# Two setup stages merged into the stages before them, and a layer norm whose variance and root stay in PSUM

## What is computed

```python
x = x + _L0_conv_ref(_gn(x), ...)      # layer 0
x = x + _L1_conv_ref(_gn(x), ...)      # layer 1

def _gn(v, G=32, eps=1e-5):            # per image, groups of 3 channels
    g = v.reshape(B_, G, C_ // G, H_, W_)
    m, s = mean(g, (2, 3, 4)), var(g, (2, 3, 4))
    return ((g - m) / sqrt(s + eps)).reshape(v.shape)

def _layernorm(x, w, b):               # over the 96 channels of a pixel
    return (x - m) / sqrt(v + EPS) * w + b

# L0: tok = windows of _gn(x); y = _layernorm(tok, norm1_w, norm1_b); q, k, v = y @ wq, y @ wk, y @ wv; ...
# L1: value, feat = 1x1 convolutions of _gn(x); centers = mean of feat over quarters of eight regions;
#     every pixel goes to the most similar centre of its region and head; aggregate, distribute, project
```

## Time and profile before

| | us |
|---|---|
| runs, median (lowest to highest) | 6937.62 (6933.67 to 6956.9) |
| profiled execution | 6937.03 |
| its span, first to last instruction | 6935.3 |
| group norm statistics (0 to the last aggregation) | 138.2 |
| attention setup and spreading of scale and shift, until the first load of the layer norm | 31.5 |
| first load of the layer norm to its first instruction on ACT | 15.3 |
| layer norm, first instruction on ACT to the first load of the attention | 448.5 |
| cluster setup, its first DMA to the cluster stage's first | 46.4 |

### The profile page before, as it was taken

How to read it: one execution, slowest core, us unless ns; L and a number is a source line. 1 busy time by engine, 2 the same in 40 slices (tenths; PEclk the granted TensorE clock), 3 DMA queues, 4 the chain that set the end, 5 groups by cost and what they waited for, 6 DMA issues and landing times. The chain is left out here.

```text
span 6935.3 us, 135783 instructions
## 1 busy us (share of the span) xinstructions
PE 6015.5 (87%) x51768; PEld 3118.6 (45%) x51768; DVE 5209.9 (75%) x7712; ACT 3497.3 (50%) x5182; POOL 2286.0 (33%) x4080
## 2 busy tenths in 40 slices
PE   0885999999999999999999689989998666578887
PEld 0332555555555555555555233335555111066663
DVE  7686888888888888888888455558887445456666
ACT  0553666666666666666666356644443111144431
POOL 0343455555554555555554656610000000000000
PEclk9997999999999999999999799999999788789987
DMA  7786344444444444444443598888987999835667
GB/s 306 192 240 179 72 106 101 101 104 106 103 108 100 103 109 102 105 101 101 107 96 71 146 269 235 237 288 345 345 341 266 283 314 316 249 90 167 189 183 248
DMA packets 761666, 1252.65 MB, mean 181 GB/s; under 512 B 159364, under 2 KB 477828, under 8 KB 730948
## 3 DMA queue, kind: packets, MB, share of 16 engines
q1 hardware_dynamic: 700532, 1090.77, 55.8%
q10 hardware_dynamic: 54560, 111.50, 5.3%
q0 software_dynamic: 5936, 41.68, 1.7%
HBM read 680.81 MB, written 508.40 MB: 171 GB/s over the span
## 5 line engine op out<-in xcount | busy, mean ns | idle before, releaser
L801 DVE TENSOR_REDUCE at_mz<-at_ps 128x4 bf16<-128x1024 f32 x1444 | 1772.3, 1227 | 105.3 <-PE at_ps L720 80.3
L668 ACT ACTIVATE at_E<-at_ps 128x1024 f32<-128x1024 f32 x1444 | 1399.4, 1021 | 382.6 <-PE at_ps L732 368.0
L732 PE MATMUL at_ps<-at_qaug,at_k 32*128 32x256 f32 x11552 | 830.0, 401 | 23.7 <-DVE at_qaug L842 23.7
L743 PE MATMUL at_ps<-at_E,at_vaug 128*32 128x256 f32 x11552 | 774.3, 385 | 5.5
L1282 PE MATMUL cv_ps<-cv_yin,cv_band 128*128 128x384 f32 x2304 | 745.4, 486 | 26.2 <-DMA cv_yin<-y_mlp 26.2
L1302 DVE TENSOR_TENSOR cv_yin<-cv_gl,cv_yin 64x384 f32<-64x384 f32 x1152 | 637.6, 553 | 150.3 <-ACT cv_gl L1293 142.4
L732 PEld LDWEIGHTS at_ps<-at_qaug,at_k 32*128 32x128 f32 x11552 | 523.0, 184 | 494.1 <-issue 384.5
L590 POOL TENSOR_TENSOR at_share<-at_rden,t_share 128x8 f32<-128x8 f32 x722 | 148.5, 206 | 1445.5 <-DVE at_rden L812 1445.5
L1282 PEld LDWEIGHTS cv_ps<-cv_yin,cv_band 128*128 128x128 f32 x2304 | 436.1, 189 | 335.7 <-DMA cv_yin<-y_mlp 27.1
L720 PE MATMUL at_ps<-at_k,at_q 32*128 32x256 bf16 x5776 | 574.2, 275 | 8.9 <-DMA at_k<-at_packed 7.4
L1293 ACT ACTIVATE cv_gl<-cv_ps,cv_bias 128x384 f32<-128x384 f32 x576 | 335.1, 582 | 435.8 <-PE cv_ps L1282 435.8
(11 more groups left out here) (217 smaller groups left out, 9596.0 us busy)
## 6 DMA issues: line engine op xcount, KB each, us to landing
cv_yin<-y_mlp SPq DMA_DIRECT2D x48, 2340.0 KB, 14.8
s_mlp<-cv_yin SPq DMA_DIRECT2D x48, 2340.0 KB, 8.4
at_rows_in<-y_attention SPq DMA_DIRECT2D x76, 768.0 KB, 6.1
gn_xin<-in_x SPq DMA_DIRECT2D x16, 3072.0 KB, 23.2
ln_xin<-in_x SPq DMA_DIRECT2D x192, 256.0 KB, 7.4
y_attention<-ln_xin SPq DMA_DIRECT2D x192, 256.0 KB, 3.8
cl_xu<-x SPq DMA_DIRECT2D x128, 384.0 KB, 3.6
at_xr<-in_x SPq DMA_DIRECT2D x68, 672.0 KB, 5.7
```

What stands on the lines that cost most here:

```text
L668: act.activation(E[:, m % 2, 2 * p:2 * p + 2, :], psum[:, 2 + 2 * p:4 + 2 * p, :], ACT.Exp).then_inc(exp_done, 1)
L732: i = pe.matmul(psum[:, 2 + h, TOK * j:TOK * j + TOK], k[rows, n % 2, tokens(w, 128 * j, 128)], qaug[rows, m % 2, :], start=True, stop=True)
L743: i = pe.matmul(pv_ps[32 * h:32 * h + VC, 0:TOK], vaug[:, m % 2, z, h, :], E[:, m % 2, h, z * TOK:(z + 1) * TOK], start=(z == 0), stop=(z ...
L801: dve.tensor_reduce(mz[:, m % 2].rearrange("p j (h c) -> p h j c", c=32)[:, 2 * p:2 * p + 2, :, DQ], psum[:, 0:2, :].rearrange("p h (j n) ...
```

## The change

1. Buffers, weights and the early loads of the layer norm are shared (norm_tables). The group norm's statistics are taken in the layer norm's own six tiles; the 16 loads of attention_setup go on ACT's queue inside group_norm_statistics, and SP issues the first two tiles of the layer norm there (LN_EARLY). The first image is aggregated in the middle.
2. gn_scale and gn_shift are spread over the partitions by three matmuls and two DVE copies in attention_setup, instead of 24 DMAs.
3. In the layer norm the variance stays in its PSUM bank. ACT takes Ln of a pair of chunks (two banks, 1024 columns) into SBUF and writes Exp back into the same banks, and DVE scales a chunk with the bank as operand, six chunks behind the centring. DVE's copy of the variance is gone. PE sums the squares two chunks behind instead of one; POOL has three buffers.
4. fc2 no longer waits for its stores; cluster_setup's SP does. The 18 loads and the memsets of cluster_setup are issued by POOL at fc2's start.
5. In cluster_setup 64 small DVE instructions become 8, the copies of means and weights go to POOL, two of the four copies of c_value_centres to ACT.

```diff
 def group_norm_statistics(nc, x, p, vdr, t, s):
+            for k in range(LN_EARLY):
+                sp.wait_ge(taken, STEPS + k - XB + 1)
+                norm_load(sp, x, s, k)
...
+            act.wait_ge(cleared, 4)
+            for to, of in setup_weights(p, t, s):
+                act.dma_start(to, of).then_inc(s["weights_loaded"], 16)
...
+                if m % PART == PART - 1:
+                    b, n = m // PART, PART * PER
+                    dve.wait_ge(taken, m + 1)
+                    dve.bn_aggr(t["mean_var"][:, b, :], stats[:, b * n:(b + 1) * n, :]).then_inc(aggregated, 1)
 def attention_setup(nc, p, t, s):
+            pool.wait_ge(s["weights_loaded"], LOADED)
+            for grp in range(CGRP):
+                pool.tensor_copy(s["spread"][:, grp, :].rearrange("p (g c) -> p g c", g=4),
+                                 t["eye"][0:C, 32 * grp:32 * grp + 32].unsqueeze(1).to_broadcast([C, 4, 32])).then_inc(spread_done, 1)
...
-            pe.matmul(ps[0:C, 3, 0:B], t["centre"][:], t["gn_shift"][:], start=True, stop=True).then_inc(pch, 1)
+            for grp in range(CGRP):
+                m = pe.matmul(ps[:, 3, 4 * grp:4 * grp + 2 * B], s["spread"][:, grp, :], t["gn"][:].rearrange("p a b -> p (a b)"), start=True, stop=True)
...
+            for b in range(B):
+                half = slice(64 * b, 64 * b + 64)
+                link(dve.tensor_copy(s["affine"][half], ps[half, 3, 0:4 * CGRP].rearrange("p (s a b) -> p a s b", a=2, b=B)[:, :, :, b]))
 def layer_norm(nc, x, y, p, t, s):
+    PAIR, PAIRS = 2, 3
+    LAG = PAIR * PAIRS
...
-                for g in range(4):
-                    for to, of in ((scale, t["gn_scale"]), (shift, t["gn_shift"])):
-                        sp.dma_start(to[32 * g:32 * g + 32, grp:grp + 1], of[32 * grp:32 * grp + 32, g // 2:g // 2 + 1]).then_inc(w_loaded, 16)
...
             def variance(n):
                 pe.wait_ge(sq_done, n + 1)
-                if n >= 2:
-                    pe.wait_ge(var_out, n - 1)
+                if n >= LAG:
+                    pe.wait_ge(z_done, n - LAG + 1)
...
+            for n in range(N + 2):
                 if n < N:
                     mean(n)
-                if n:
-                    variance(n - 1)
+                if n >= 2:
+                    variance(n - 2)
...
+            def roots(j):
+                banks = slice(root(PAIR * j), root(PAIR * j) + PAIR)
+                act.wait_ge(var_done, PAIR * (j + 1))
+                act.activation(logs[:, j % 2], psum[:, banks, :], ACT.Ln, bias=t["eps5"][:]).then_inc(log_done, 1)
+                act.wait_ge(log_done, j + 1)
+                act.activation(psum[:, banks, :], logs[:, j % 2], ACT.Exp, scale=-0.5).then_inc(rs_done, 1)
+            for n in range(XH_AHEAD):
+                affine(n)
+            for n in range(N + LAG):
+                if n + XH_AHEAD < N:
+                    affine(n + XH_AHEAD)
+                j = (n - LAG + PAIR) // PAIR
+                if n % PAIR == 0 and 0 <= j < N // PAIR:
+                    roots(j)
...
-            def variance(n):
-                dve.wait_ge(var_done, n + 1)
-                dve.tensor_copy(rs[:, n // PER % 3, cols(n)], psum[:, 2 + n % 2, :]).then_inc(var_out, 1)
+            def normalised(n):
+                dve.wait_ge(rs_done, n // PAIR + 1)
+                dve.tensor_tensor(chunk(n), chunk(n), over_groups(psum[:, root(n), :]), ALU.mult).then_inc(z_done, 1)
+            for n in range(N + LAG):
+                if n < N:
+                    centred(n)
+                if n >= LAG:
+                    normalised(n - LAG)
+def norm_load(queue, x, s, k):
+    i = (k + GN_TILES) % XB
+    for grp in range(CGRP):
+        for g in (0, 2, 1, 3):
+            queue.dma_start(s["xin"][32 * g:32 * g + 32, i, grp, :], norm_rows(x, k, g, grp)).then_inc(s["loaded"][i], 16)
 def fc2(nc, p, xs, sdr, x1, tab, t, s, ctx):
-            for u in range(XA):
-                sp.wait_ge(stored[u], 16 * XLOADS * len(range(u, NTILE, XA)))
+        @block.gpsimd
+        def _(pool):
+            for to, of in setup_loads(p, t, s):
+                pool.dma_start(to, of).then_inc(s["loaded"], 16)
 def cluster_setup(nc, p, tab, t, s, x1_stored):
+            for arrived, count in x1_stored:
+                sp.wait_ge(arrived, count)
...
+            pool.wait_ge(stage, 4)
+            for q in range(NREG):
+                pool.tensor_copy(xmq[:, q].rearrange("p e (i j) -> p e i j", j=2),
+                                 quarters(xm, q).unsqueeze(1).to_broadcast([C + 1, CH_HEADS, 2, 2])).then_inc(spread_done, 1)
+            for b in range(B):
+                pool.tensor_copy(t["rhs"][:, 4 * b:4 * b + 4, 0:2 * C], wfv[:, b, :].unsqueeze(1).to_broadcast([C + 1, 4, 2 * C])).then_inc(spread_done, 1)
...
-                for e in range(CH_HEADS):
-                    link(dve.tensor_scalar(ctr[:, q, e, :].rearrange("p (i j) -> p i j", j=2), quarters(cn), heads[:, e:e + 1], None, ALU.mult))
-                    link(dve.tensor_copy(xmq[:, q, e, :].rearrange("p (i j) -> p i j", j=2), quarters(xm)))
+                last = dve.tensor_tensor(ctr[:, q].rearrange("p e (i j) -> p e i j", j=2),
+                                         quarters(cn, q).unsqueeze(1).to_broadcast([C, CH_HEADS, 2, 2]),
+                                         heads[:].unsqueeze(2).unsqueeze(3).to_broadcast([C, CH_HEADS, 2, 2]), ALU.mult)
```

More of the change, by code:

```diff
@@ L60, in group_norm_statistics @@
         lines = ctx.enter_context(nc.sbuf_tensor("gn_lines", [C, 2, PHASES, 2, 2, SHIFTS, 2], F32))
-        loaded = [ctx.enter_context(nc.semaphore(f"gn_loaded{i}")) for i in range(NBUF)]
+        loaded = s["loaded"]
         taken = ctx.enter_context(nc.semaphore("gn_taken"))
@@ L313, in variance @@
                 pe.wait_ge(sq_done, n + 1)
-                if n >= 2:
-                    pe.wait_ge(var_out, n - 1)
+                if n >= LAG:
+                    pe.wait_ge(z_done, n - LAG + 1)
                 for grp in range(CGRP):
-                    m = pe.matmul(psum[:, 2 + n % 2, :], ones[:], sq[:, n % 2, grp, :], start=(grp == 0), stop=(grp == CGRP - 1))
+                    m = pe.matmul(psum[:, root(n), :], ones[:], sq[:, n % SQ, grp, :], start=(grp == 0), stop=(grp == CGRP - 1))
@@ L1313, in fc2 @@
     XA = 3
-    with ExitStack() as ctx:
+    with ExitStack() as block_ctx:
         def sb(nm, shape, dt=F32):
@@ L1466, in _ @@
                 store(act, k, 1)
-            for u in range(XA):
-                act.wait_ge(stored[u], 16 * XLOADS * len(range(u, NTILE, XA)))
+    return [(stored[u], 16 * XLOADS * len(range(u, NTILE, XA))) for u in range(XA)]
 CH_HEADS, CH_DIM = 4, 24
@@ new lines, in cluster_setup @@
+def cluster_setup(nc, p, tab, t, s, x1_stored):
+    with ExitStack() as ctx:
+        folded = s["folded"]
+        pick = s["pick"]
+        bsum = s["bsum"]
+        stat = s["stat"]
+        avg = s["avg"]
+        sq = s["sq"]
+        sd = s["sd"]
+        eps = s["eps"]
+        scale = s["scale"]
+        shift = s["shift"]
+        group = s["group"]
+        heads = s["heads"]
+        same = s["same"]
+        fv_t = s["fv_t"]
+        fv_b = s["fv_b"]
+        f_col = s["f_col"]
+        f_nat = s["f_nat"]
+        alpha = s["alpha"]
+        wfv = s["wfv"]
+        xm = s["xm"]
+        xmq = s["xmq"]
+        cf = s["cf"]
+        cs = s["cs"]
+        cn = s["cn"]
+        ctr = s["ctr"]
+        psum = s["psum"]
+        loaded = s["loaded"]
+        ones_set = s["ones_set"]
@@ L1578, in _ @@
             act.activation(cs[:].rearrange("p b n -> p (b n)"), psum[0:C, 4, 0:B * NBK], ACT.Sqrt).then_inc(ach, 1)
+            act.wait_ge(pch, 5)
+            for j in range(2):
+                rows_j = slice(32 * j, 32 * j + EM)
+                act.activation(t["value_centres"][rows_j].rearrange("p f c -> p (f c)"), psum[rows_j, 6, 0:NREG // 2 * C], ACT.Copy).then_inc(ach, 1)
+            act.wait_ge(ach, 4)
         @block.tensor
         def _(pe):
-            pe.wait_ge(loaded, 16 * len(loads))
+            pe.wait_ge(loaded, LOADED)
             pe.wait_ge(folded_done, 2)
@@ L1645, in _ @@
             staged()
-            dve.wait_ge(loaded, 16 * len(loads))
+            dve.wait_ge(loaded, LOADED)
             dve.wait_ge(pch, 2)
@@ L2123, in program @@
         t = cluster_tables(nc, ctx)
-        fc2(nc, p, xs, sdr, x1, tab)
-        cluster_setup(nc, p, tab, t)
+        with ExitStack() as inner:
+            s = setup_tables(nc, inner)
+            x1_stored = fc2(nc, p, xs, sdr, x1, tab, t, s, inner)
+            cluster_setup(nc, p, tab, t, s, x1_stored)
         cluster(nc, x1, out, t, slot_loaded, slot_stored, slot_counts)
```

319 lines of the change are left out of this document (137 added, 182 removed).

## The result

The changed kernel takes 6767.0 us (median of 4 runs, 6761.1 to 6786.6) against 6941.5 (6933.7 to 6956.9) for the kernel before on the same chip: a ratio of 0.9753, 95% interval 0.9735 to 0.9771.

What follows compares the result with a forecast made beforehand. DVE bounds the layer norm before, PE and DMAs close behind; afterwards the DMAs, at 22.5 us a tile. Gains of 114.6 before the attention and 27 in fc2 and cluster setup: 6937.0 - 141.6 = 6795.4, predicted 6796, range 6768 to 6832.

Steps and rivals of the forecast that it cites:

- Setup and early loads: Ahead of the layer norm: weight wait 9.1, spreading DMAs and ones matrix 15.9, first tile's wait 15.3 go; 40.3 us together.
- A gain of 0 for the aggregation: Group norm statistics: moving one aggregation of 2.7 us into the statistics gains 0, bounds -1 and 2.7.
- Durations: Layer norm instruction times: DVE's scaling 1.75 us, Ln and Exp about 1.05 each, ACT 18 a tile.
- The slow scaling rival: Layer norm: DVE's product with PSUM still takes 3.9 us beside POOL; 18 us more, 6813; chance 0.13.
- Fill: Layer norm, from ACT's first instruction to the first store: 54 us, against 74.7 before.
- Tail: From the last tile's first instruction on ACT to the attention's first load: 50 us, against 48.9 before.
- The DMAs as the bound: Layer norm: DMAs take over as the bound at 22.5 us a tile, 270 us for twelve; forecast case, chance 0.52.
- The DMA rival: Layer norm: DMAs keep up with PE, 20.6 us a tile; 23 us less, 6772; chance 0.15.
- The round trip: Layer norm: load-to-store loop takes 40 us against 45 for two tiles; rival: it rules, 29 more, 6824, chance 0.17.
- fc2 and cluster setup: From fc2's end to the cluster stage: 29.2 us less gross, net gain 27, bounds 24 and 30.
- the forecast's 0.7: Cluster setup: DVE loses 0.7 us, bounds 0 and 3, as centre placements with two SBUF operands meet POOL's copies.
- The 1.6 us for loads inside fc2: fc2: 462 KB of added setup loads cost 1.6 us, at a DMA share of 1.00 and 298 GB/s.

Runs made afterwards that it cites:

- the bf16 kernel: Changed kernel with squares in bf16 and a bf16 ones matrix for the variance matmuls, loads still four tiles ahead: 6746.0 us against 6938.3 for the kernel before (0.9725).
- the swap: Kernel before with only DVE's order changed, centring chunk n before scaling chunk n-8: 6960.2 us against 6938.3 (1.0032).

## Why the prediction was right, and where it was not

*Setup and early loads*: forecast 40.3 us, measured 38.2. The waits and the spreading DMAs went as read. The 2.1 us that are missing lie behind the statistics: the 9.1 us wait for the weights was counted as gone whole, but 1.9 of it stay, until the setup's block begins, and the chain behind it takes 6.9 us for 6.5. Without the early loads that entry wait was 0.5. A gain of 0 for the aggregation was right: the other aggregation's 2.7 went into the wait for the last statistics load, 3.99 for 1.04 before. The prediction charged 1.5 us there for the added weights but nothing for the early tiles; taking these out gave 2.2 back.

*Durations*: scaling 1.75 us forecast, 1.75 measured; Ln and Exp 1.05 each, measured 1.11 and 1.03; ACT's tile 18.0, and the tiles of the kernel with bf16 squares and loads five ahead, where ACT is busy all the time, stand 17.9 apart. The slow scaling rival is out. The value was in part luck, though. The reason given for it was the root's place in PSUM, and the run with the roots in SBUF has 1.79 too, since DVE's order changed as well, which the prediction did not weigh. The page SBUF — State Buffer of the Trainium skill, section "Who interferes with whom", was cited for it: two SBUF inputs contend with GpSimd and the second blocks. The runs agree, and the weight is on "second": with both inputs in SBUF it was DVE at 3.43 to 3.92, or POOL at 4.06 to 4.19, by the order in which they began; with one input in PSUM neither was slowed (1.75 and 2.75).

*Fill*: 54 forecast, 51.3 measured. *Tail*, last tile's first instruction on ACT (450.01) to the attention's first load: 50 forecast, 52.9 measured.

*The DMAs as the bound*: this step failed. It took 22.8 us for a tile's stores and loads from one stretch of the kernel before, at a share of 0.94, and read a share near 1 as work that can't go faster. The tiles went at PE's 20.6, so the stretch up to the last tile's first instruction took 252.0 for 270. The same traffic later went at 17.9. Nothing in the changed kernel but PE sets its pace. The DMA rival, at 6772 and a chance of 0.15, had the pace right, though its reason, a share of 0.94, says little: a share shows that transfers are in flight, not at what rate. In that stretch of the kernel before, 8.5 us of stores went at 288 GB/s and a share of 0.90, then 14.3 of loads at 256 and 0.96. In the changed kernel it is 357 and then 257, at 1.01 and 0.99. So the loads alone are no quicker, and the gain lies where the stores are issued. In steps of 2 us, the first while stores are in flight, the second when the last of them is through:
```profile
346.00:348.00 2.00, 2.00 (x6) 0.84 (x5) 1.36 (x1) 1.89 (x3) 2.00 (x1) 1.00 1.03 430
358.00:360.00 2.00, 2.00 (x6) 0.86 (x5) 0.61 (x1) 1.97 (x3) 0.82 (x1) 1.00 1.05 242
```
ACT got the tile loaded last at 346.11, so at 430 GB/s stores alone are in flight, and at 242 loads alone. My reading, which no run tests: before, the loads had landed (438.7) when the stores began (441.1), and these went as fast as SP issued them, an estimated 331 GB/s (12 of 256 KB in 9.5 us); in the changed kernel stores pile up behind loads for some 4 us and then drain. Rows of the kernel before spoke against me: fc2 moved 298 GB/s at 1.00, at which a tile's 24 transfers of 256 KB take 21.1 us, and the statistics' loads of 3 MB, which the prediction did not look at, moved 436 at 1.01:
```profile
60.00:95.00 35.00, 0.00 (x0) 0.00 (x0) 33.77 (x57) 0.00 (x0) 0.00 (x0) 1.00 1.01 436
```

*The round trip*: its 40 us were near (40.8 in one pair and 41.9 on average, both in the bf16 kernel), and it did not rule here since PE is just above it.

*fc2 and cluster setup*: 29.2 gross forecast for the stretch behind fc2, 29.8 measured. The first matmul comes 9.9 after the last group of stores began against 21.1; the chain behind it takes 18.3 against 36.9. The contention came, at another instruction: not the eight products for the centres (0.77 for all; POOL had finished by then, at 5913.4) but one product with both inputs in SBUF ahead of them (L1713), 0.88 us for 0.19 before, while POOL copied. That it is as much as the forecast's 0.7 is chance. The 1.6 us for loads inside fc2 can't be seen under that stage's scatter; fc2 was 13.7 shorter, unforeseen and, as told, unexplained.

*Sum*: forecast 6795.4 (the case with the DMAs as the bound, chance 0.52, which did not come true); 2.0 more for the setup, 17.8 less for the layer norm, 13.7 less for fc2, 2.8 less behind it, 2.5 less over the other stages: 6760.6, and the profiled execution took 6761.1. Of the 34.8 us, 17.8 are the failed step. The 13.7 of fc2 are no merit or fault of the reasoning: they decide whether a time falls just inside or just outside the range, as the two measurements of the changed kernel show.

## What to carry to other kernels

A share of busy DMA time near 1 is not a capacity. Before a stage is called DMA bound, look for the highest rates that other stretches of the same trace move, and take from them the least time that the traffic could need (6.3 MB a tile at 436 GB/s: 14.4 us, an estimate, since those loads have another shape); or add a tile of prefetch and see. When two limits lie within a few per cent, removing one only shows the other: the swap made DVE cheaper and POOL dearer, and the kernel became 0.3% slower. An engine's wait for loads need not cost anything, and the cheapest test is to prefetch one tile more.

## What the hardware showed that I had not expected

- The cost of two engines wanting SBUF can be moved: DVE 3.43 and POOL 2.75 us in one order, DVE 1.75 and POOL 4.19 in the other, a sum of 6.2 and 5.9.
- The DMA engines showed a share of 0.98 to 1.01 at 257, 300, 303, 345, 357 and 436 GB/s.
- A stage that moves data at a share of 1 all the time (fc2) differed by 7 and by 13 us between two executions of the same kernel, with the attention's start ahead of it repeating within 2.1.
